# A perceiver layer on one core: inputs transposed on the host, a short prologue with the rest of it moved into the first steps, a written-out expert loop

## What is computed

```python
x = x + xattn(layernorm(x), ctx, Wq, Wk, Wv, Wo, bo)   # 16 heads of 64, softmax over 257 rows
x = x + attn(layernorm(x), mix_k, mix_v, mix_r, W_key, W_value, W_receptance, W_output,
             time_decay, time_first)                   # a decayed running sum over 32 positions
x = x + ffn(layernorm(x), Wr, br, W1, b1, W2, b2)      # argmax picks 1 of 8 experts per token
```

## Time and profile before

| | us |
|---|---|
| median of 3 runs | 1046.47 |
| lowest, highest | 1040.83, 1046.96 |
| the profiled execution: its own time | 1041.88 |
| its span | 1039.8 |
| busy in the span: PE, PEld | 908.2, 764.9 |
| busy: DVE, ACT, POOL | 809.0, 712.0, 700.8 |
| granted TensorE clock, mean | 0.936 |

### The profile page before, as it was taken

How to read it: one execution, slowest core, us unless ns; L and a number is a source line. 1 busy time by engine, 2 the same in 40 slices (tenths; PEclk the granted TensorE clock), 3 DMA queues, 4 the chain that set the end, 5 groups by cost and what they waited for, 6 DMA issues and landing times.

```text
span 1039.8 us, 31371 instructions
## 1 busy us (share of the span) xinstructions
PE 908.2 (87%) x9098; PEld 764.9 (74%) x9099; DVE 809.0 (78%) x2325; ACT 712.0 (68%) x2040; POOL 700.8 (67%) x1210
## 2 busy tenths in 40 slices
PE   3799999999999999999999999999998374078885
PEld 3678888888888888888888888888886273056664
DVE  5778879898989889898989899898988557045553
ACT  2488888778787887878787788778874113056663
POOL 4366687877778787877778787878785404724544
PEclk9999999999999999999999999999999556579888
DMA  6000100000001000000001000000000930111110
GB/s 190 11 17 18 33 18 18 17 18 17 17 16 31 15 15 15 15 15 15 15 16 29 17 15 15 15 15 15 16 3 1 182 105 29 52 46 45 43 43 14
DMA packets 46505, 32.35 MB, mean 31 GB/s; under 512 B 6518, under 2 KB 44065, under 8 KB 46448
## 3 DMA queue, kind: packets, MB, share of 16 engines
q1 hardware_dynamic: 44144, 27.38, 10.9%
q0 software_dynamic: 2304, 4.25, 1.3%
HBM read 24.62 MB, written 7.52 MB: 31 GB/s over the span
## 4 chain that ended last, share of the span: by engine, by line
PE 38%; POOL 31%; issue 17%; ACT 5%; DVE 4%; POOLq 1%; DMA 1%; ACTq 1%; SPq 1%; DVEq 0%
POOL Pn L774 13%; PE bank L388 6%; PE bank L411 6%; PE bank L433 4%; PE bank L1299 4%; PE bank L400 3%; POOL chi L756 3%; PE bank L426 3%; PE bank L1314 2%; POOL sorted_rows L1103 2%; ACT Pe L560 2%; POOL sraw L856 2%; POOL cT L766 2%; POOL e12p L781 1%; ACT hr L1189 1%
## 5 line engine op out<-in xcount | busy, mean ns | idle before, releaser
L774 POOL TENSOR_TENSOR Pn<-Pe,rsum 128x1028 f32<-128x1028 f32 x128 | 243.0, 1899 | 132.1 <-DVE rsum L644 132.1
L560 ACT ACTIVATE Pe<-bank,nmax 128x257 f32<-128x257 f32 x512 | 242.9, 480 | 17.4 <-DVE nmax L630 11.0
L630 DVE TENSOR_REDUCE nmax<-bank 128x1 f32<-128x257 f32 x512 | 203.4, 418 | 42.2 <-PE bank L388 38.9
L388 PE MATMUL bank<-cT,qh 96*128 96x257 f16 x1024 | 185.3, 275 | 9.4 <-issue 3.9
L552 ACT ACTIVATE Th<-bank 128x512 f16<-128x512 f32 x256 | 141.4, 595 | 49.9 <-PE bank L433 49.9
L624 DVE TENSOR_TENSOR Tl<-bank,Th 128x512 f16<-128x512 f32 x256 | 174.3, 682 | 0.5 <-ACT Th L552 0.4
L433 PE MATMUL bank<-identf,Pn 128*128 128x128 f32 x1024 | 147.0, 273 | 0.0
L388 PE MATMUL bank<-cT,ql 96*128 96x257 f16 x512 | 139.5, 272 | 0.0
L433 PEld LDWEIGHTS bank<-identf,Pn 128*128 128x128 f32 x1024 | 114.7, 142 | 5.6
L388 PEld LDWEIGHTS bank<-cT,qh 96*128 96x128 f16 x1024 | 93.7, 98 | 21.5 <-issue 9.5
L560 ACT ACTIVATION_READ_ACCUMULATOR Pe<-bank,nmax 128x1 f32 x512 | 107.3, 210 | 0.0
(11 more groups left out here) (238 smaller groups left out, 2541.8 us busy)
## 6 DMA issues: line engine op xcount, KB each, us to landing
raw<-in_ctx_dram SPq DMA_DIRECT2D x32, 384.0 KB, 3.3
sorted_rows<-fill SPq DMA_DIRECT2D x1, 2620.0 KB, 21.8
xs<-sorted_rows SPq DMA_DIRECT2D x40, 65.5 KB, 1.8
R<-in_x_dram SPq DMA_DIRECT2D x4, 512.0 KB, 5.8
Z<-last_rows SPq DMA_DIRECT2D x128, 2.2 KB
w1r<-in_L_ffn_W_dram SPq DMA_DIRECT2D x8, 256.0 KB, 6.0
w2fr<-in_L_ffn_W_dram SPq DMA_DIRECT2D x8, 256.0 KB, 6.4
out_dram<-yout,idx POOLq DMA_INDIRECT x40, 2.3
```

The lines of the kernel that those rows point to most:

```text
L388: last = nc.tensor.matmul(bank[SB[t]][:, 0:M], w[:, par, b, t * P:(t + 1) * P], cT[:, s4, c, 0:M], start=(k == 0), stop=(k == 2))
L560: nc.scalar.activation(Pe[:, n_par(j + 1), t, :], bank[SB[t]][:, 0:M], ACT.Exp, bias=nmax[:, n_par(j + 1), t:t + 1], accum_out=sums[:, n_p ...
L630: nc.vector.tensor_reduce(nmax[:, n_par(j + 1), t:t + 1], bank[SB[t]][:, 0:M], AX.X, ALU.max, negate=True).then_inc(s_nmax, 1)
L774: nc.gpsimd.tensor_tensor(Pn[:, par, :, :], Pe[:, par, :, :], rsum[:, par, :].unsqueeze(2).broadcast_to([P, QT, M]), ALU.mult)\
```

## The change

The host lays out the inputs: `ctxT` (a second, transposed copy of the context, with its 257th column), all weights transposed, the per-channel vectors as one array. Hence:

- `pe_ctxT`, `dve_cT` and `pool_last` go. In each step ACT writes the high half of `cT` for n+4 from `rawT` in SBUF, and POOL the low half (`pool_cT`). SP loads `rawT` ahead of `raw`.
- The prologue keeps the statistics and norm of the first quarter and the first unit of x, the four groups of A, and q of four sequences. Four products of B, seven units, three quarters' statistics and the tables go to steps n=-1 to 20 (`*_early`), which the first written-out iterations hold.
- The reciprocal deviation of the first norm is made by POOL (`pool_rstd1`), not by ACT's Sqrt and DVE.
- PE runs 16, 10 and 6 products of the identity with itself (`pe_warm`) at three waits of the prologue.
- The FFN weights come transposed, in four pairs of DMAs; ACT and DVE split them from SBUF.
- `over_tiles` writes out all tiles; `pk` holds 8 digits, each engine reads a pack once and takes a tile's digit once.

```diff
-        def pe_ctxT(n, s8, s4):
...
-        QB = (0, 1, 6, 0)
+        QB = (0, 1, 2, 3)
...
+        UNIT = {4: 1, 6: 2, 8: 3, 10: 4, 12: 5, 14: 6, 20: 7}
+
+        def pe_early(n):
+            n = n_static(n)
+            if n is not None and -1 <= n < 3:
+                k = n + 1
+                wait(nc.tensor, s_ql, n + 6)
+                wait(nc.tensor, s_wvo, 32)
+                for a in range(4):
+                    lo, pair = (k % 2) * D, k // 2 * 4 + a
+                    last = nc.tensor.matmul(bank[3][0:CC, a * C:(a + 1) * C], wvT[lo:lo + D, pair, :],
+                                            wo_r[lo:lo + D, pair, :], start=True, stop=True)
+                last.then_inc(s_ab, 1)
+            if n in UNIT:
+                wait(nc.tensor, s_ql, n + 6)
+                wait(nc.tensor, s_xn1, UNIT[n] + 1)
+                pe_norm_T(UNIT[n] % 2, 3, s_x1T)
+
+        def act_early(n):
...
+            if n in UNIT:
+                act_x1h(UNIT[n])
...
+        def dve_moments1(groups):
+
+            for k in groups:
+                if k % GQ == 0:
+                    nc.vector.wait_ge(s_x[k // GQ], 16)
+                nc.vector.bn_stats(stats[:, k, :], X[:, k, :]).then_inc(s_ln, 1)
+            for k in groups:
+                nc.vector.wait_ge(s_ln, k + 1)
+                nc.vector.bn_aggr(mv1[:, k, :], stats[:, k, :]).then_inc(s_mv1, 1)
...
+        def dve_early(n):
+            n = n_static(n)
+            if n in (0, 1):
+                dve_moments1(range(GQ + CT * n, GQ + CT * n + CT))
+            if n in (4, 6):
+                dve_moments1(range(2 * GQ + CT * (n - 4) // 2, 2 * GQ + CT * (n - 4) // 2 + CT))
+            if n in (8, 10):
+                dve_moments1(range(3 * GQ + CT * (n - 8) // 2, 3 * GQ + CT * (n - 8) // 2 + CT))
+            if n is not None and n + 1 in UNIT:
+                dve_norm1(UNIT[n + 1])
...
+        def dve_early_end(n):
...
+            if n in UNIT:
+                dve_x1l(UNIT[n])
...
+        def pool_early(n):
+            n = n_static(n)
+            if n in (2, 6, 10):
+                pool_rstd1({2: 1, 6: 2, 10: 3}[n])
+            if n in UNIT:
+                pool_bo(UNIT[n])
+            if n == 3:
+                pool_tables()
...
         def pe_mix_free(it, j):
+            prev = n_static(it)
+            prev = None if prev is None else 8 * it + j - 1
+            if prev is not None and -1 <= prev < 3:
+                wait(nc.tensor, s_abl, 6 + prev)
+            if prev in UNIT:
+                wait(nc.tensor, s_x1l, UNIT[prev] + 1)
...
             for t in range(QT):
-                if t == 2 and exists(n + 2):
-                    act_cT(n + 2, (j + 2) % 4)
+                if t == 2 and exists(n + 4):
...
+                    act_cT(n + 4, (j + 4) % 4, ((j + 4) // GB) % NP2, (j + 4) % GB)
...
+        def act_cT(n, s4, par, b):
+            wait(nc.scalar, s_S, QT * (n - 3))
+            nc.scalar.activation(cT[:, s4, 0, 0:M], rawT[:, par, b, :], ACT.Copy).then_inc(s_cTh, 1)
...
-        def pool_last(n, s4):
-
-            wait(nc.gpsimd, s_S, QT * (n - 3))
-            nc.gpsimd.tensor_copy(cT[:, s4, :, MC * P:M], c256T[:, :, bass.ds(n, 1)]).then_inc(s_lcol, 1)
+        def pool_cT(n, s4, par, b):
+
+            wait(nc.gpsimd, s_cTh, n + 1)
+            nc.gpsimd.tensor_tensor(cT[:, s4, 1, 0:M], rawT[:, par, b, :], cT[:, s4, 0, 0:M], ALU.subtract)\
+                .then_inc(s_cT, 1)
...
         def over_tiles(eng, step, routed=True):
-            def block(it):
-                pack = eng.value_load(pk[0:1, bass.ds(it, 1)], min_val=0, max_val=E ** NV - 1) if routed else None
-                for u in range(1 - UN, 1):
-                    step(it, u, lambda v: (pack // E ** (v + 5)) % E)
...
-            with eng.Fori(3, NT // UN) as it:
-                block(it)
...
+            def expert(s):
+                q, digit = divmod(s, PK)
+                if q not in packs:
+                    packs[q] = eng.value_load(pk[0:1, q:q + 1], min_val=0, max_val=E ** PK - 1)
+                if s not in experts:
+                    experts[s] = (packs[q] // E ** digit) % E
+                return experts[s]
+
+            for it in range(NT // UN + 2):
                 for u in range(1 - UN, 1):
+                    step(it, u, lambda v: expert(UN * it + v))
...
+            load_x(0)
+            sp.dma_start(wkT[:, :, :], WkT.rearrange("(a p) c -> p a c", p=P)).then_inc(s_w, 16)
+            sp.dma_start(wqT[:, :, :], WqT.rearrange("(a p) c -> p a c", p=P)).then_inc(s_w, 16)
+            sp.dma_start(c256[:, :], ctx[:, LAST, :]).then_inc(s_c256, 16)
             load_ctx(0, 0)
             load_ctx(1, 1)
...
+        def pe_warm(count):
+
+            for _ in range(count):
+                nc.tensor.matmul(bank[2][:, 0:P], identf[:, :], identf[:, :], start=True, stop=True)
...
             pe.wait_ge(s_const, 2)
+            pe_warm(16)
+            pe.wait_ge(s_w, 32)
+            for k in range(4):
...
+                last.then_inc(s_ab, 1)
+            pe_warm(10)
+            pe.wait_ge(s_xn1, 1)
+            pe_norm_T(0, 3, s_x1T)
+            pe_warm(6)
+            pe.wait_ge(s_abl, 4)
+            pe.wait_ge(s_x1l, 1)
+            for c in range(GB):
+                pe_q(c, c, slice(0, P), QB[c], 0)
             pipeline(nc.tensor, pe_step)
```

More of the change, by code:

```diff
@@ L42, in mark, with perceiver_layer_kernel @@
         ins.then_inc(self.sem, 1)
-def perceiver_layer_kernel(nc, x, ctx, Wq, Wk, Wv, Wo, bo, mix_k, mix_v, mix_r, W_key, W_value,
-                           W_rec, W_out, decay, first, Wr, br, W1, b1, W2, b2, out):
+def perceiver_layer_kernel(nc, x, ctx, ctxT, WqT, WkT, WvT, Wo, bo, mixT, W4T, WrT, br, W1T, b1T_d, W2T, b2, out):
     B, N, C = x.shape
     _, M, CC = ctx.shape
-    HD = Wq.shape[1]
+    HD = WqT.shape[0]
     H = 16
@@ new lines, in act_early @@
+        def act_early(n):
+            n = n_static(n)
+            if n is not None and -1 <= n < 3:
+                k = n + 1
+                wait(nc.scalar, s_ab, 5 + k)
+                nc.scalar.activation(heads(Bhi, k), bank[3][0:CC, :].rearrange("p (a c) -> p a c", a=4), ACT.Copy)\
+                    .then_inc(s_abh, 1)
+            if n in UNIT:
+                act_x1h(UNIT[n])
+            if n == 5:
+                wait(nc.scalar, s_w2, 32)
+                nc.scalar.activation(nlw[:, :], dcy, ACT.Exp).then_inc(s_texp, 1)
+                wait(nc.scalar, s_m["zero"], 5)
+            if n == 7:
+                wait(nc.scalar, s_tdve, 2)
+                wait(nc.scalar, s_tab, 1)
+                nc.scalar.activation(apw[:, :], tt[:, :], ACT.Exp, scale=nlw2[:, 0:1]).then_inc(s_texp, 1)
@@ new lines, in act_x1h, with dve_x1l @@
+        def act_x1h(u):
+            wait(nc.scalar, s_x1T, u + 1)
+            nc.scalar.activation(x1h[:, T * u:T * (u + 1)], bank[3][:, :], ACT.Copy).then_inc(s_x1h, 1)
+        def dve_x1l(u):
+            wait(nc.vector, s_x1h, u + 1)
+            nc.vector.tensor_tensor(x1l[:, T * u:T * (u + 1)], bank[3][:, :], x1h[:, T * u:T * (u + 1)],
+                                    ALU.subtract).then_inc(s_x1l, 1)
+        def dve_moments1(groups):
[6 more added lines that the diff above has]
+                nc.vector.bn_aggr(mv1[:, k, :], stats[:, k, :]).then_inc(s_mv1, 1)
@@ new lines, in _ @@
+                    last = nc.tensor.matmul(bank[4 + k][:, a * CC:(a + 1) * CC], wqT[lo:lo + D, pair, :],
+                                            wkT[lo:lo + D, pair, :], start=True, stop=True)
+                last.then_inc(s_ab, 1)
+            pe_warm(10)
[4 more added lines that the diff above has]
+            pe.wait_ge(s_x1l, 1)
+            for c in range(GB):
+                pe_q(c, c, slice(0, P), QB[c], 0)
@@ L1276, in _ @@
                                  start=True, stop=True).then_inc(s_cnt, 1)
-            pe.wait_ge(s_w3r, 32 * E)
             pe.wait_ge(s_f["lg"], CH)
-            for k in range(2 * E):
-                wait(pe, s_w3l, k - 3)
-                for f in range(FC):
-                    src = w1r[:, k // 2, f, :] if k % 2 == 0 else w2fr[:, k // 2, f * P:(f + 1) * P]
-                    last = nc.tensor.transpose(bank[4 + k % 4][:, f * P:(f + 1) * P], src, identf[:, :])
-                last.then_inc(s_w3T, 1)
             pe.wait_ge(s_te, 1)
@@ L1365, in _ @@
+            dve_x1l(0)
+            for c in range(GB):
+                dve_q(c, 0, c, QB[c])
             pipeline(nc.vector, dve_step)
```

472 lines of the change are left out of this document (209 added, 263 removed).

## The result

The changed kernel takes **1029.79 us** (median of 4 runs, 1028.92 to 1033.20) against 1043.86 for the kernel before beside it: ratio 0.9869, 95% interval 0.9827 to 0.991. It is faster by 14 us, 1.3%; forecast were 29, and the time lies just above the range of 992 to 1029.

A forecast was written before the change was run, and what follows sets the result against it. PE looked like the only bound, though three places in an iteration already waited for others. Prologue -29, early steps +10, loop 0, expert loop -10: -29 from 1041.88, so 1013; forecast 1014 us, range 992 to 1029.

The forecast's parts named there:

- Prologue: Stretch before the first score product: first score at 22.5 us (20 to 28) instead of 51.44, gain 29 (24 to 31).
- Early steps: Attention steps n=-1 to 20, which take the work moved out of the prologue: loss 10 us (4 to 16).
- The 0.22 saved per step: Attention steps: PE loses four transposes, 0.225 us per step; counted inside the early steps' loss of 10.
- Rival B: Early steps: moved work hurts more, 2.5 us in 11 places rather than 0.9, clock low until 28; 1029, up to 1036; chance 0.11.
- Loop: Steady attention iterations: PE's saving and POOL's later xn nearly cancel, 0 us (-13 to +10).
- Rival C: Attention loop: POOL bounds every step, from 0.87 us more per step; at 1.25, +41 us, 1054; chance 0.04.
- Rival A: Attention loop: PE's saving goes through as xn isn't later, 0.9 to 1.8 us per iteration, 988 to 1001; chance 0.22.
- Expert loop: The 40 expert tiles at the end: written out, with fewer register loads, gain 10 us (4 to 15).

The follow-up runs named there:

- no_warm: The changed kernel without the 32 products of the identity on TensorE; 1028.5 us, ratio 0.985.
- z_later: The changed kernel with GpSimd's memset of Z behind the three context preparations instead of ahead of them; 1024.8 us, ratio 0.982.
- b_first: The changed kernel with the four B products and their drains back in the prologue; 1025.9 us, ratio 0.982.
- light: The changed kernel with most of GpSimd's early work (rstd chains of quarters 1 to 3, bo additions of units 1 to 7) left out; 1025.1 us, ratio 0.982.
- norm_quarter: The changed kernel with the norm of units 2 to 7 over one of four tiles; 1026.8 us, ratio 0.982.
- ct_small: The changed kernel with GpSimd's new subtraction over 16 of 257 columns from n=4 on; 1012.7 us, ratio 0.970.
- xn_first: The changed kernel with GpSimd's context preparation behind the mixing work in steps j=5 and j=6, nothing left out; 1013.1 us, ratio 0.972.

## Why the prediction was wrong, by its steps

**Prologue: right, partly by luck.** First score 20.67 (22.5 taken, 20 to 28), gain 30.8. The A groups took neither 2.02 nor 1.11 each but 0.68: the upper level, which the identity products gave (no_warm: 1.22 each without them), and four groups in a row, which the sum didn't have. Against that stood 2.5 us of a norm held by a memset, which it didn't have either (0.9 of it on the first score, by z_later). By the rule of the Trainium skill (TensorE: Matmul & The Clock Gate, Part 1), that sustained activity releases the lower level, the first score was to come at 20. The change's trace agrees with it; the one of before still does not, with groups of 2.02 in 20 us in which TensorE was busy for 19.63.

**Early steps: the step that failed.** Forecast +10 (4 to 16) over n=-1 to 20, measured +18.5 to n=12 and +19.9 to n=20. The B products were priced well (4.4; b_first 3.1 by n=4). The seven units were bounded by VectorE, with "a norm of 1.11 on DVE" ahead of rsum and steps "at about 5.9". GpSimd's share was not in the sum: three chains of 3.15 us and seven additions of bo of 1.18 between two Pn, although the change's list names `pool_rstd1` and the prologue's sum has one chain at 2.4. The step to n=12 took 8.41 with them and 6.10 without. Nor was the subtraction, which these steps pay and the sum had covered by "The 0.22 saved per step is in it". To n=20, one by one, with the 1.8 of the clock at n=8 and 9 taken off each and the 1.2 at n=1 given back to light and norm_quarter: B products 3.5 us, GpSimd's early work 3.0, norms 3.1, subtraction 4.1, by the profiles of b_first, light, norm_quarter and ct_small. That is 13.7 (an estimate, for whether they add was not run), with 1.8 of clock; some 4 stay open. Rival B named 2.5 us per moved piece, by bank 3 and nmax; measured are 19.9 over 11 pieces, 1.8 each, and the mechanism is mostly another. Its sum also had 10 where 11 times 1.6 is 17.6: added right, with or without its 5 for the clock, it comes to 1032 to 1037.

**Loop: right in its parts, wrong in the net.** Subtraction 0.683 for 0.67; wait for xn 1.46 for "1.1 or more". (Its net, 0.67 less 0.24, is 0.43 and not the 0.47 of the sum; measured 0.44.) But "j=0 to j=3: 0.9 gained, since POOL is back in time there" did not happen: the step with oT, mdx and xm grew from 6.73 to 7.23 us, with a Pn that starts without a wait. I had read 7.1 us of waits per iteration in the earlier trace rows as slack; they stand in other steps. In before three of eight Pn start without a wait, in the change four. Net +0.41 per iteration; with the steps from n=20 to 32 (+4.1) the loop lost 8 us where the sum had 0. Rival C, "POOL becomes the bound of every step", came true in half the steps, at x = 0.44 (0.683 less 0.240) where its condition said 0.87; that condition divided the same 7.1 us evenly over eight steps. The 1.45 us that it gave the subtraction occurred in one step of the change (at 220.56), not in every one.

**Rival A** was wrong for the change. Its condition, an xn that isn't later, is what xn_first brings about, and then the period is 46.61: 0.36 below before, where A had 0.9 to 1.8.

**Expert loop: right.** -8.4 in this profile, -9 to -12 in the others, forecast -10.

Open: what makes the granted clock fall in one kernel and not in another that has done the same work up to there, and why the last stretch varies by 3 us with the same code. The four kernels timed on one of the chips have 241.7 to 242.3 there, the thirteen on three others 239.2 to 240.7; the change has 242.7.

## What to carry to other kernels

When work moves from a prologue into a pipeline, price it on every engine of the step, GpSimd's small instructions first: seven of 8 elements were 3 us. Slack of an engine is a matter of each step, not of the iteration: mark which instances of a periodic instruction start without a wait before giving that engine more. Before moving work off the busiest engine, look for what it waits for at one place; putting one result first in its producer's queue gave 10.4 us from n=32 on, the most of any single edit that leaves nothing out. And before two profiles are compared step by step, compare their granted clock over the same steps: one fall of it was 1.84 us here, as much as most of the parts that were being measured.
